# A decoder layer on one core: the attention loop's order, its division, its leads and an extra matmul

## The chip, the cores and the metric

The kernel runs on one core of a Trainium2 chip. The metric is the device time of one execution in microseconds; the time of a kernel is the median of several executions.

## The reference, cut to what matters

Input `x` and context are 8 batches of 256 tokens of 256 features (2048 tokens in all). Three sublayers follow each other, each with a layer norm ahead of it and a residual sum behind it.

```
x = x + mixer(layernorm(x))          # linear, depthwise conv, silu, decays by cumprod/cumsum, gates
q = layernorm(x) @ WQ + bQ; k = ctx @ WK + bK; v = ctx @ WV + bV      # 16 heads of 16
scores = where(causal, q k^T * 0.25, -inf); out = softmax(scores) @ v
x = x + out @ WO + bO
xn = layernorm(x); probs = softmax(xn @ router_w.T)        # 8 experts, top 2
rank = place of the pair within its expert; keep = rank < 641
h = silu(buf @ w1[e]); y = h @ w2[e]
x = x + (sum over k of k_prob * y[pair]) + xn
```

## The kernel before

The program has two parts with a barrier of all engines between them.

`mixer_and_projections` goes over four blocks (`NBLK`) of 512 tokens and makes the mixer's output, and the queries, keys and values of the attention. Large products are split: each fp32 operand is held as a high and a low part, and three products are summed (`split_product`, L101). Queries and keys are stored to HBM (`qd`, `kd`), values too (`vd`).

`attention_route_experts` has a loop over steps `t` (`for t in range(END)`), written out for each engine, and behind it the experts. The attention is cut into 16 groups `g` (`GR`: a batch and a half of its heads), each of three units: queries of the first 128 tokens with their keys (s = 0), and two units of later queries with all keys. There are 48 units (`NS`). Each unit is worked on twice:

- As a *lead*: `mask` (L243) and `scores` (L268) write scores of a unit `u` into `lead.sbank`, and VectorE's `maxima` (L282) reduces them to the negative row maxima's source. After the third unit of a group `turn_maxima` (L290 to L295) splits and transposes the maxima, SP stores them to HBM (`store_maxima`, L214) and loads them back as two more rows of the laid queries (`load_maxima`, L222).
- As a *turned* unit: `turned_mask` (L243) and `turned` (L1504) write the transposed scores less their maxima into `tbank`, ScalarE's `exps` (L1397) makes the exponentials, and `weigh` (L1522) multiplies with the values into `obank`.

The lead runs ahead of the turned unit by `LEAD` steps: in step `t` unit `u = t + LEAD` is masked and scored. The first `LEAD` units are done at the end of the mixer part, by `unit(u)` on TensorE and `maxima` on VectorE, placed by hand among the last block's products. `mask` waits for the maxima of the unit before it (`A["nm"]`), since there is one score buffer. The operands of a group are laid out in SBUF by four DMAs (`lay`, L207) into one of four places (`ITEMS`), when the last turned unit of the group four before has been read.

In the loop TensorE's order in a step is: turned mask of t, mask of u, turned scores of t, scores of u, then what is due (output projection `project` L1538 for a batch, the transposes `x3_turn` L1550, router `logits` L1560, `ranks` L1570), then `weigh(t - 1)`. What is due follows from constants: a batch's work at step `PROJECT + 6 b`, a block's at `constant + 12 i`.

VectorE's order is: maxima, turning of the maxima in each third step, `divide` of a group in each third step (transpose L1663, reciprocal L1665, multiplication L1667, transpose L1671), `x2` with the residual sum (L1678) and the statistics (L1681), `offset`, `choose` (best two of the router's logits, the gates), `place` (ranks to slots), and in each sixth step a piece of expert 0's second weights (`split_w2`, L1735, L1737). GpSimd adds the output bias at the start (L1317), takes inverse roots (`power`, L1321), adds the base (L1326), scatters the tokens to `disp` (L1335) and splits pieces of expert 0's first weights (L1342). ScalarE has the exponentials and, among them, normalised rows, copies and `high_w1`.

SP issues all other DMAs in one order: for each group from 2 on `lay(g + 2)`, `store_maxima(g)`, `load_maxima(g)`; behind group 3's the whole weights of expert 0 (two DMAs of 1 MB, L1264, L1267), behind group 6's those of expert 1; values (L233) and the stores of the base (L1278) at others.

Behind the loop the experts run one after the other, with TensorE's products L101 and L1613.

## Time and profile before

| what | value |
|---|---|
| median of 3 runs | 759.76 us (755.79 to 762.71) |
| profiled execution: its own time | 765.45 us |
| profiled execution: span | 763.7 us, 12738 instructions |
| mean granted TensorE clock | 0.866 |
| TensorE busy | 631.9 us, 83% |
| TensorE weight loads | 537.9 us, 70% |
| VectorE busy | 511.6 us, 67% |
| ScalarE busy | 340.3 us, 45% |
| GpSimd busy | 323.1 us, 42% |

The span is that of one profiled execution, from its first to its last instruction; its own time is a little longer. Busy shares are means over stages with different limits: the mixer to about 277 us, the attention loop to 440 us, the routing of the last block to about 475 us, the experts to the end. In the rows below a line begins with its start and its length in us; L and a number is the line of the kernel; in brackets stands how long the engine was idle before it and what ended that. PE is TensorE (PEld its weight loads), DVE VectorE, ACT ScalarE, POOL GpSimd, SPq the DMA issues of SP. The granted clock is a share of 2.4 GHz.

### The profile page before, as it was taken

What the parts mean: (1) busy time and instruction counts of PE and PEld (TensorE: products, weight loads), DVE (VectorE), ACT (ScalarE), POOL (GpSimd) and SP (SyncE); (2) the same over time, 40 slices, a digit from 0 to 9 for tenths busy, and PEclk for the clock granted to TensorE, in tenths of its full rate; (3) what the DMA queues carried; (4) which work ended last, traced back from release to release, by engine and by line L of the source; (5) the groups of instructions that cost most, each with busy time, mean ns of one, the idle gap of its engine ahead of it and who ended that gap; (6) DMA issues with size and microseconds to landing.
All of it is one profiled execution on the core that took longest, in us unless ns stands there. A gap on an engine that the chain in (4) does not pass through costs nothing.

```text
span 763.7 us, 12738 instructions
## 1 busy us (share of the span) xinstructions
PE 631.9 (83%) x4600; PEld 537.9 (70%) x4600; DVE 511.6 (67%) x1049; ACT 340.3 (45%) x658; POOL 323.1 (42%) x304
## 2 busy tenths in 40 slices
PE   3687989979976678679899751799999999999991
PEld 2465878867764645456566531699999999999991
DVE  5686787795785665775777741287777778777630
ACT  4565663742612123342342620356566555655540
POOL 1235433251430040020150637145867767677665
PEclk9798999999998665986676955699999999999996
DMA  9201305845229535775555201604253453521123
GB/s 285 80 26 43 99 28 158 258 117 151 70 54 269 120 86 102 221 206 119 120 130 136 83 11 42 214 1 148 29 164 57 132 148 46 162 27 19 19 30 41
DMA packets 60542, 81.16 MB, mean 106 GB/s; under 512 B 10188, under 2 KB 45015, under 8 KB 60481
## 3 DMA queue, kind: packets, MB, share of 16 engines
q1 hardware_dynamic: 51264, 72.55, 34.1%
q0 software_dynamic: 9216, 7.81, 7.2%
q8 instruction: 36, 0.59, 0.3%
q14 instruction: 26, 0.21, 0.1%
HBM read 48.01 MB, written 34.10 MB: 108 GB/s over the span
## 4 chain that ended last, share of the span: by engine, by line
PE 34%; issue 13%; POOL 6%; DMA 5%; SPq 2%; DVE 2%; ACT 1%; POOLq 0%; DVEq 0%
PE w_bank L1613 16%; PE w_bank L101 14%; POOL disp L1335 3%; DMA l_lo<-kd 3%; POOL out L1359 2%; PE l_scores L1582 1%; DMA md<-l_mt 1%; SPq L207 1%; PE a_shared L1538 1%; SPq L1259 1%; POOL l_lo L1348 1%; DMA w_rows<-disp 1%; DVE l_nm L282 1%; DMA out<-w_y,w_to 1%; POOL w_w1l L1342 0%
## 5 line engine op out<-in xcount | busy, mean ns | idle before, releaser
L1761 DVE SCALAR_TENSOR_TENSOR w_v<-w_th,w_bank 128x324 f32<-128x324 f32 x128 | 62.9, 491 | 71.1 <-ACT w_th L1430 69.8
L1613 PE MATMUL w_bank<-w_w2h,l_hi 128*108 128x256 f32 x384 | 108.6, 283 | 0.5 <-POOL l_lo L1348 0.5
L1613 PE MATMUL w_bank<-w_w2h,l_lo 128*108 128x256 f32 x384 | 107.7, 281 | 0.0
L1613 PE MATMUL w_bank<-w_w2l,l_hi 128*108 128x256 f32 x384 | 107.7, 280 | 0.0
L1430 ACT ACTIVATE w_th<-w_bank 128x324 f32<-128x324 f32 x128 | 56.5, 442 | 100.4 <-PE w_bank L101 100.3
L1348 POOL TENSOR_TENSOR l_lo<-w_v,l_hi 128x324 fp32r<-128x324 f32 x64 | 56.3, 880 | 91.8 <-ACT l_hi L1436 91.8
L1397 ACT ACTIVATE a_pr<-a_turned 128x1024 f32<-128x1024 f32 x48 | 49.1, 1023 | 96.8 <-PE a_turned L1504 96.8
L101 PE MATMUL w_bank<-l_hi,w_w1h 128*128 128x324 f32 x256 | 80.8, 316 | 1.1 <-ACT l_hi L1425 1.1
L101 PE MATMUL w_bank<-l_hi,w_w1l 128*128 128x324 f32 x256 | 80.9, 316 | 0.0
L1359 POOL DMA_INDIRECT out<-w_y,w_to x48 | 75.3, 1569 | 13.2 <-issue 9.9
L101 PE MATMUL w_bank<-l_lo,w_w1h 128*128 128x324 f32 x256 | 80.8, 316 | 0.0
L282 DVE TENSOR_REDUCE l_nm<-l_scores 128x4 f32<-128x1024 f32 (+1 forms) x48 | 58.1, 1211 | 33.1 <-PE l_scores L268 33.1
L1342 POOL TENSOR_TENSOR w_w1l<-w_s,w_w1h 128x256 fp32r<-128x256 f32 x64 | 57.0, 891 | 42.7 <-ACT w_w1h L1419 42.6
L1737 DVE TENSOR_TENSOR w_w2l<-w_s,w_w2h 128x256 fp32r<-128x256 f32 x64 | 65.5, 1024 | 2.2
L1613 PEld LDWEIGHTS w_bank<-w_w2h,l_hi 128*108 128x108 f32 x384 | 66.0, 172 | 0.9 <-issue 0.9
L1613 PEld LDWEIGHTS w_bank<-w_w2l,l_hi 128*108 128x108 f32 x384 | 65.9, 172 | 0.0
L1613 PEld LDWEIGHTS w_bank<-w_w2h,l_lo 128*108 128x108 f32 x384 | 65.9, 172 | 0.0
L1436 ACT ACTIVATE l_hi<-w_v 128x324 fp32r<-128x324 f32 x128 | 60.4, 472 | 12.0 <-DVE w_v L1761 11.1
L101 PEld LDWEIGHTS w_bank<-l_hi,w_w1h 128*128 128x128 f32 x256 | 49.1, 192 | 1.4 <-ACT l_hi L1425 1.4
L101 PEld LDWEIGHTS w_bank<-l_lo,w_w1h 128*128 128x128 f32 x256 | 49.2, 192 | 0.0
L101 PEld LDWEIGHTS w_bank<-l_hi,w_w1l 128*128 128x128 f32 x256 | 49.1, 192 | 0.0
L478 POOL TENSOR_TENSOR m_gl<-m_acc,m_gh 128x512 fp32r<-128x512 f32 x16 | 24.5, 1533 | 36.8 <-ACT m_gh L599 36.8
(229 smaller groups left out, 1541.6 us busy)
## 6 DMA issues: line engine op xcount, KB each, us to landing
w_s<-in_L_ffn_w SPq DMA_DIRECT2D x16, 1024.0 KB, 5.3
l_hi<-qd SPq DMA_DIRECT2D x32, 192.0 KB, 4.4
l_lo<-kd SPq DMA_DIRECT2D x32, 192.0 KB, 4.9
disp<-c_blank SPq DMA_DIRECT2D x8, 658.1 KB
w_rows<-disp SPq DMA_DIRECT2D x8, 658.1 KB
kd<-l_qkh SPq DMA_DIRECT2D x16, 256.0 KB, 4.7
vd<-m_vf SPq DMA_DIRECT2D x4, 1024.0 KB, 7.0
qd<-l_qkh SPq DMA_DIRECT2D x16, 256.0 KB, 5.0
```

Of the source, the lines that this page charges most:

```text
L101: mm = pe.matmul(out, a, b, start=first and n == 0, stop=last and n == 3 * len(parts) - 1)
L282: dve.tensor_reduce(dst, src, AX.X, ALU.max).then_inc(A["nm"], 1)
L478: pool.tensor_tensor(out[:, n, :], src, high[:, n, :].bitcast(F32), ALU.subtract).then_inc(S[name], 1)
L1342: pool.tensor_tensor(w1_piece(w1l, f), w1_piece(s1[e % 2], f), w1_piece(w1h, f).bitcast(F32), ALU.subtract)\
L1348: pool.tensor_tensor(hl[:, g % 3, half(1)], v[:, n % 4, :], hh[:, g % 3, half(1)].bitcast(F32), ALU.subtract)\
L1359: pool.indirect_dma_start(out=out, out_offset=bass.IndirectOffsetOnAxis(ap=to[:, e % 3, t:t + 1], axis=0), in_=y[e % 2][:, t, :], in_offse ...
L1397: act.activation(pr[n % 3][:, :], tbank[:, :], ACT.Exp, scale=SCALE).then_inc(A["exp"], 1)
L1430: act.activation(th[:, n % 2, :], hb[n % 3][:, 0:HALF], ACT.Tanh, scale=0.5).then_inc(F["th"], 1)
L1436: act.activation(hh[:, g % 3, half(u)], v[:, n % 4, :], ACT.Copy).then_inc(F["hh"], 1)
L1613: mm = pe.matmul(eb[t // 2][0:SP_, (t % 2) * D:(t % 2 + 1) * D], a[:, g % 3, s], w2_piece(b, f), start=f == 0 and t % 2 == 0 and n == 0, s ...
L1737: dve.tensor_tensor(w2_piece(w2l, f), w2_piece(s2[e % 2], f), w2_piece(w2h, f).bitcast(F32), ALU.subtract)\
L1761: dve.scalar_tensor_tensor(v[:, n % 4, :], th[:, n % 2, :], 1.0, hb[n % 3][:, 0:HALF], ALU.add, ALU.mult).then_inc(F["v"], 1)
```

## The change

- `LEAD` is 6 instead of 7. The six leading units get other places: unit 0 stood ahead of the last block's first products (`queries` of block 2, the projection `w2`), now it stands behind `w2`, and each of the others one place on; VectorE's maxima and their turning likewise. In SP's order laying group 1 moves behind the stores of block 2's queries. GpSimd takes the inverse root of block 2 ahead of four memsets instead of behind them.
- `divide` is cut: `invert` on VectorE (transpose, reciprocal), the multiplication on GpSimd (`divide`), and `turn_back` on VectorE one step later. One output bank instead of two; the x3 transposes get a bank of their own (`xbank`).
- The routing pieces get new steps, and the statistics and the gates are cut off from `x2` and `choose`.
- `keep_warm`: at the head of 36 of the 48 steps (all with t mod 12 not in 8, 9, 10) TensorE does one matmul of bf16 identity by 512 columns into `xbank`, whose result nothing reads.
- Expert 0's weights come in eight pairs of pieces of 128 KB (`first_weights`) in the groups with odd numbers, expert 1's behind group 14's maxima. The loads of the router's and the output projection's weights move behind group 2's maxima, and the last queries are stored in two halves with the maxima's load between them.

```diff
-LEAD = 7
+LEAD = 6
@@ mixer, sync
                     if i == NBLK - 1:
                         lay(sp, A, S, lead, qd, kd, 0)
-                        lay(sp, A, S, lead, qd, kd, 1)
+                lay(sp, A, S, lead, qd, kd, 1)
+                load_values(sp, A, S, lead, vd, 0)
                 lay(sp, A, S, lead, qd, kd, 2)
-                load_values(sp, A, S, lead, vd, 0)
                 lay(sp, A, S, lead, qd, kd, 3)
@@ mixer, tensor
-                    if i == NBLK:
-                        unit(0)
...
                     if last:
                         w2(i - 1)
                     if i == NBLK:
-                        unit(1)
+                        unit(0)
...
-                unit(6)
+                unit(5)
@@ mixer, vector
-                maxima(dve, A, lead, 6)
-
+                maxima(dve, A, lead, 5)
+                turn_maxima(dve, A, own, lead, 1)
@@ loop
-    PROJECT, BOTH, NORM, TURN, LOGITS, RANKS, SEND = 8, 14, 16, 18, 22, 24, 26
+    PROJECT, STATS = 8, 10
+    POWER, OFFSET, NORM, TURN, BASE, LOGITS = 17, 18, 19, 20, 21, 22
+    CHOOSE, RANKS, WEIGHTS, PLACE, SEND = 25, 26, 27, 31, 32
@@ sync
+                def first_weights(f):
+                    ge(sp, F["w1h"], f - 1)
+                    sp.dma_start(w1_piece(s1[0], f), w1[0:D, f * P:(f + 1) * P].rearrange("(k p) f -> p k f", p=P))                        .then_inc(F[f"p1_{f % 2}"], 16)
+                    ge(sp, F["w2l"], f - 1)
+                    sp.dma_start(w2_piece(s2[0], f), w2[f * P:(f + 1) * P, :]).then_inc(F[f"p2_{f % 2}"], 16)
...
-                    if g == 3:
-                        weights(0)
-                    if g == 6:
...
+                    if g % 2 == 1:
+                        first_weights(g // 2)
+                    if g == GR - 2:
                         weights(1)
@@ gpsimd
+                def divide(g):
+                    pool.wait_ge(A["po"], g + 1)
+                    pool.wait_ge(A["rc"], g + 1)
+                    ge(pool, A["o"], g)
+                    pool.tensor_tensor(on[:, :].rearrange("p (j h v) -> p h j v", h=2, v=HD), po[:, :, :, 0:HD],
+                                       rc[:, :, :].unsqueeze(3).to_broadcast([P, 2, 2 * 4, HD]), ALU.mult).then_inc(A["on"], 1)
@@ tensor
+                def keep_warm(t):
+
+                    if t % 12 in (8, 9, 10):
+                        return
+                    if t >= 23:
+                        pe.wait_ge(S["xt"], 2 * ((t - 23) // 12 + 1))
+                    pe.matmul(xbank[:, :], c["identb"][:, :], c["identb"][:, :].unsqueeze(1).to_broadcast([P, 4, P]),
+                              start=True, stop=True, skip_group_check=True)
...
                 for t in range(END):
                     u = t + LEAD
                     if t < NS:
+                        keep_warm(t)
                         turned_mask(t)
@@ vector
-                def divide(g):
+                def invert(g):
+                    dve.wait_ge(A["pv"], 3 * g + 3)
+                    ge(dve, A["on"], g)
+                    dve.transpose(po[:, :, :, :].rearrange("p h j r -> p (h j r)"), obank[:, :]).then_inc(A["po"], 1)
+                    dve.wait_ge(A["po"], g + 1)
+                    dve.reciprocal(rc[:, :, :], po[:, :, :, HD]).then_inc(A["rc"], 1)
+
+                def turn_back(g):
...
+                    dve.wait_ge(A["on"], g + 1)
                     ge(dve, S["y"], b - 1)
                     dve.transpose(ot[:, k, (b % 2) * L:(b % 2 + 1) * L], on[:, :]).then_inc(A["o"], 1)
...
                     if t % 3 == 0 and 1 <= t // 3 <= GR:
-                        divide(t // 3 - 1)
+                        invert(t // 3 - 1)
+                    if t % 3 == 1 and 1 <= t // 3 <= GR:
+                        turn_back(t // 3 - 1)
```

How the instructions now stand, at three places. TensorE, a step t with t mod 3 = 1 (step 4) of the loop: `a_turned` is the turned scores' bank, `l_scores` the leads', `a_out` the weighed values'. Before:

```order
970 L243 MATMUL a_turned<-c_identb,c_laterT 128x2x64 [waits a_exp]
971 L243 MATMUL a_turned<-c_identb,c_laterT 128x2x64 x3
972 L243 MATMUL l_scores<-c_identb,c_later 128x2x64 [waits a_nm]
973 L243 MATMUL l_scores<-c_identb,c_later 128x2x64 x3
974 L1504 MATMUL a_turned<-l_hi,l_lo 128x256 x4
975 L268 MATMUL l_scores<-l_lo,l_hi 128x256 x4
976 L1522 MATMUL a_out<-a_pr,l_hi 32x256 [waits a_v_in0,a_exp]
```

and of the change:

```order
971 L1516 MATMUL a_turned_x<-c_identb 128x512
972 L243 MATMUL a_turned<-c_identb,c_laterT 128x2x64 [waits a_exp]
973 L243 MATMUL a_turned<-c_identb,c_laterT 128x2x64 x3
974 L243 MATMUL l_scores<-c_identb,c_later 128x2x64 [waits a_nm]
975 L243 MATMUL l_scores<-c_identb,c_later 128x2x64 x3
976 L1534 MATMUL a_turned<-l_hi,l_lo 128x256 x4
977 L268 MATMUL l_scores<-l_lo,l_hi 128x256 x4
978 L1552 MATMUL a_out<-a_pr,l_hi 32x256 [waits a_v_in0,a_po,a_exp]
```

The extra matmul stands between the last weighing and the turned mask that waits for the exponential, and the weighing that begins a group now waits for `a_po`, the first transpose of the group before it.

VectorE, steps 6 to 8 of the loop. Before, with the whole division behind the maxima of step 6:

```order
306 L282 TENSOR_REDUCE l_nm<-l_scores 128x2x2 [waits a_s]
307 L1663 STREAM_TRANSPOSE a_po<-a_out 128x512 [waits a_pv]
308 L1665 RECIPROCAL a_rc<-a_po 128x16 [waits r_step]
309 L1667 TENSOR_TENSOR a_on<-a_po,a_rc 128x2x8x16 [waits r_step]
310 L1671 STREAM_TRANSPOSE a_ot<-a_on 128x256 [waits r_step]
311 L282 TENSOR_REDUCE l_nm<-l_scores 128x2x2 [waits a_s]
312 L290 CAST l_mx<-l_nm 128x16 [waits a_mx,a_nm]
313 L292 TENSOR_TENSOR l_mx<-l_nm,l_mx 128x16 [waits r_step]
314 L295 STREAM_TRANSPOSE l_mt<-l_mx 128x32 [waits a_md,r_step]
315 L282 TENSOR_REDUCE l_nm<-l_scores 128x8 [waits a_s]
316 L1678 TENSOR_TENSOR g_x<-a_shared,g_x 128x512 [waits w_y,w_xb]
```

and of the change:

```order
306 L282 TENSOR_REDUCE l_nm<-l_scores 128x8 [waits a_s]
307 L1688 STREAM_TRANSPOSE a_po<-a_out 128x512 [waits a_on,a_pv]
308 L1690 RECIPROCAL a_rc<-a_po 128x16 [waits a_po]
309 L282 TENSOR_REDUCE l_nm<-l_scores 128x2x2 [waits a_s]
310 L1696 STREAM_TRANSPOSE a_ot<-a_on 128x256 [waits a_on]
311 L282 TENSOR_REDUCE l_nm<-l_scores 128x2x2 [waits a_s]
312 L290 CAST l_mx<-l_nm 128x16 [waits a_mx,a_nm]
313 L292 TENSOR_TENSOR l_mx<-l_nm,l_mx 128x16 [waits r_step]
314 L295 STREAM_TRANSPOSE l_mt<-l_mx 128x32 [waits a_md,r_step]
315 L1702 TENSOR_TENSOR g_x<-a_projected,g_x 128x512 [waits w_y,w_xb]
```

The multiplication has left VectorE, the second transpose stands a step later, and the turning of the maxima moved from the second to the third step of a group.

SP, behind group 2's maxima. Before, where `w_s` is the experts' weights and 1 MB each:

```order
108 L214 DMA md<-l_mt 4x32x32 [waits a_mx]
109 L222 DMA l_hi<-md 2x1024 [waits a_md]
110 L222 DMA l_hi<-md 2x1024
111 L1264 DMA w_s_0<-in_L_ffn_w 128x2x1024
112 L1267 DMA w_s_0<-in_L_ffn_w 128x8x256
113 L207 DMA l_hi<-qd 48x4x256 [waits a_st]
```

and of the change:

```order
111 L214 DMA md<-l_mt 4x32x32 [waits a_mx]
112 L222 DMA l_hi<-md 2x1024 [waits a_md]
113 L222 DMA l_hi<-md 2x1024
114 L1267 DMA w_s_0<-in_L_ffn_w 128x2x128
115 L1269 DMA w_s_0<-in_L_ffn_w 128x256
116 L207 DMA l_hi<-qd 48x4x256 [waits a_st]
```

The two large loads have become two small ones at the same place.

## Rows read from the trace of the kernel before

**Rows 1.** Stretches: us, us, busy PE, PEld, DVE, ACT, POOL; clock, DMA share, GB/s.
```profile
277.00:440.00 163.00, 137.11 (x1458) 90.20 (x1456) 112.50 (x267) 59.70 (x76) 40.58 (x33) 0.74 0.56 141
...
486.00:745.00 259.00, 258.53 (x1986) 257.93 (x1985) 184.94 (x367) 146.44 (x368) 169.76 (x161) 0.99 0.34 79
```

**Rows 2.** The exponentials: duration ns min/median/max, first and last start us.
```profile
L1397 ACT ACTIVATE a_pr<-a_turned x48: 1003/1023/1026, 277.5 to 439.9; 128x1024 f32<-128x1024 f32 x48
```

**Rows 3.** Waits in 277 to 440: us in total, times, longest.
```profile
PE l_scores L243 <- DVE l_nm L282: 9.3, 16, 1.1
...
PE l_scores L268 <- DMA l_lo<-kd: 5.6, 3, 2.8
...
PE a_out L1522 <- DMA l_lo<-vd: 2.0, 1, 2.0
```

**Rows 4.** Timeline of TensorE, steps at the low and at the high clock.
```profile
297.92 0.40 PE L243 MATMUL a_turned<-c_identb,c_laterT 64*128 64x128 bf16 x4
...
300.59 0.40 PE L243 MATMUL a_turned<-c_identb,c_laterT 64*128 64x128 bf16 x4
...
376.11 0.29 PE L243 MATMUL a_turned<-c_identb,c_laterT 64*128 64x128 bf16 x4
...
377.92 0.29 PE L243 MATMUL a_turned<-c_identb,c_laterT 64*128 64x128 bf16 x4 [0.31 <-ACT a_pr L1397]
379.27 0.29 PE L243 MATMUL l_scores<-c_identb,c_later 64*128 64x128 bf16 x4 [1.07 <-DVE l_nm L282]
...
379.69 0.40 PE L268 MATMUL l_scores<-l_lo,l_hi 48*128 48x256 f32 x4
...
380.97 0.39 PE L243 MATMUL a_turned<-c_identb,c_laterT 64*128 64x256 bf16 x4 [0.31 <-ACT a_pr L1397]
382.41 0.61 PE L243 MATMUL l_scores<-c_identb,c_later 64*128 64x256 bf16 x4 [1.04 <-DVE l_nm L282]
...
394.45 1.99 PE L1538 MATMUL a_shared<-w_wo,a_ot 128*128 128x256 f32 x8
...
402.53 0.61 PE L243 MATMUL a_turned<-c_identb,c_laterT 64*128 64x256 bf16 x4
...
406.10 0.40 PE L243 MATMUL a_turned<-c_identb,c_laterT 64*128 64x128 bf16 x4
```

**Rows 5.** Timeline of VectorE, the division's ends and the maxima behind it.
```profile
379.13 0.71 DVE L1663 STREAM_TRANSPOSE a_po<-a_out 128x512 f32<-128x512 f32 x1
...
380.80 0.45 DVE L1671 STREAM_TRANSPOSE a_ot<-a_on 128x256 f32<-128x256 f32 x1
381.16 1.19 DVE L282 TENSOR_REDUCE l_nm<-l_scores 128x4 f32<-128x1024 f32 x1
```

**Rows 6.** Timelines of VectorE and TensorE, the mixer's end, ahead of w2.
```profile
237.51 1.28 DVE L954 TENSOR_TENSOR m_xal<-m_ssm,m_xah 128x512 fp32r<-128x512 f32 x2
...
240.03 1.12 PE L268 MATMUL l_scores<-l_lo,l_hi 48*128 48x128 f32 x8 [3.62 <-DMA l_lo<-kd]
```

**Rows 7.** SP's issues around group 4's maxima, and its waits for all groups.
```profile
305.22 1.36 SPq L207 DMA_DIRECT2D l_hi<-qd  x2
...
307.95 0.55 SPq L214 DMA_DIRECT2D md<-l_mt  x1
316.58 0.57 SPq L222 DMA_DIRECT2D l_hi<-md  x2
...
SPq L222 <- DMA md<-l_mt: 58.0, 15, 8.4
```

**Rows 8.** Two operations by line: duration ns min/median/max, first and last start.
```profile
L1667 DVE TENSOR_TENSOR a_on<-a_po,a_rc x16: 424/425/2236, 290.0 to 443.5; 128x256 f32<-128x256 f32 x16
...
L1342 POOL TENSOR_TENSOR w_w1l<-w_s,w_w1h x8: 720/734/877, 310.0 to 453.2; 128x256 fp32r<-128x256 f32 x8
```

**Rows 9.** Timeline of VectorE, the gates of the last block.
```profile
462.25 0.18 DVE L1710 TENSOR_SCALAR w_one<-w_ex 128x4 f32<-128x4 f32 x1
...
462.95 0.17 DVE L1716 TENSOR_TENSOR w_x<-w_wr,w_x 128x4 f32<-128x4 f32 x1
```

149 lines of the change are left out of this document (74 added, 75 removed).

## The prediction

> **What bounds the kernel now.** I read the table of stretches first, then the waits and the timelines of the attention loop. The loop runs from 277 to 440 us, and in it TensorE is busy 137 of 163 us at a mean granted clock of 0.74 [rows 1]. The clock has two levels, 1.2 and 2.4 GHz, so 0.74 is (1 - 0.74) / 0.5 = 52% of the time at the lower one: 85 us. The experts behind it (486 to 745 us) run at 0.99 with TensorE busy throughout; the change leaves them alone. So the time has to come from the loop, from the mixer's end ahead of it, or from the routing tail behind it.
>
> The 48 exponentials start between 277.5 and 439.9 us [rows 2], 162.4 / 47 = 3.46 us a step, and last 1.02 us each: ScalarE is not the bound. One step is a ring of four engines. TensorE masks and makes scores, VectorE takes their maxima, TensorE may only then mask the next scores; and since its queue is in order, the turned scores of the next step, and so the next exponential, stand behind that mask. TensorE's own waits are 9.3 us for VectorE, 5.6 us for keys and 2.0 us for values [rows 3].
>
> At the high clock a narrow step is short: mask at 376.11, next mask at 377.92, 1.81 us, of which the last 0.31 us is the wait for the exponential [rows 4]. At the low clock the same step goes from 297.92 to 300.59, 2.67 us, without any wait. In the step after 377.92 the mask waits 1.07 us, because the division (from 379.13) and the maxima stand one behind the other on VectorE: the division's four operations fill 379.13 to 381.25 [rows 5]. After two steps with waits of 0.31, 1.07 and 1.04 us the matmuls at 382.41 are at the lower clock [rows 4]. The waits thus cost twice: as waits, and as a slow array for the steps behind them.
>
> **The mixer's end.** Unit 0 stood ahead of the projection w2 in TensorE's queue and held it 3.62 us for its keys, until 240.03; it ended at 241.15. The inputs of w2 are ready when VectorE's two subtractions from 237.51 end, 1.28 us later, at 238.79 [rows 6]. Unit 0 now stands behind w2, so w2 starts 241.15 - 238.79 = 2.4 us earlier, and the chain to the barrier with it. Given back: the six leading units end with both VectorE's maxima and their turning (three small operations like those of [rows 9], taken at 0.6 us), and a turning also stands ahead of the normalisation (0.6 us). Net -1.0 us, bounds -3 and +1. One unit fewer ahead of the loop costs nothing in it by itself: its last steps had no scores to make, now the last six rather than seven.
>
> **Waits for transfers.** 5.6 + 2.0 = 7.6 us [rows 3]. The laying of an item waits for the turned scores of the item four before it, as before, and its scores now come one step later (six leading units), one more step of 2 to 3 us for the transfer. The two loads of 2 MB each for experts 0 and 1 stood in the queue ahead of it: with one ahead, the small store of maxima issued at 307.95 let its load go only at 316.58, 8.6 us, where SP's fifteen waits of this kind are 3.9 us in the mean [rows 7]. Expert 0's weights now come in eight pairs of pieces, and expert 1's at the last items but two. I take -6 us. New costs: fourteen more issues on SP, and the last maxima store behind expert 1's 2 MB, +1 us. Together -5.0 us, bounds -8 and +3.
>
> **VectorE's pieces.** The division's multiplication goes to GpSimd, its second transpose one step on; statistics, choice, gates and placing get steps of their own; and with six leading units the turning of the maxima falls in a step without division. A step's surplus beside the maxima falls from 2.1 us [rows 5] to about 0.4 to 1.0 us, which fits beside TensorE's mask, turned scores and scores. Not in all steps: choice, the split of w2 and the placing still overrun. Of 9.3 us of waits I take half, -4.5 us, bounds -9 and 0. On GpSimd a subtraction of the same 128x256 takes 0.73 us against 0.42 us on VectorE [rows 8]; it has a whole step there and hides. A single output bank replaces two: the next item's first weighing waits for the first transpose, which is a step earlier.
>
> Here a rule of the Trainium skill speaks against the change: SBUF — State Buffer, section "SBUF: two separate sides", says that VectorE and GpSimd share one port pair, which an instruction holds alone, so that a GpSimd operation blocks VectorE's operations with two SBUF inputs. The trace agrees that such a thing occurs: this division's multiplication takes 0.425 us in the median and 2.236 us at most [rows 8]. By the rule sixteen divisions of 0.73 us on GpSimd could return up to 12 us; but what stands behind the reciprocal on VectorE is the maxima, which read PSUM.
>
> **The filler.** 48 steps less 12 skipped (three in each twelve) are 36 matmuls of 512 columns. None like it is in the trace. The nearest are the masks, in bf16 too: four of 256 columns, two and two side by side, stream 512 columns in 0.61 us at the low clock (402.53) and in 0.39 us at the high one (380.97) [rows 4], the end of the last one included. Half the clock costs 0.22 us more, so the columns themselves are 0.22 us at the high and about 0.43 us at the low clock, which I take; bounds 0.2 and 0.6. In the 0.31 us wait of a fast narrow step it costs nothing. In steps where TensorE is the bound, as when the output projection runs (1.99 us at the high clock [rows 4]), it is added: 8 fast steps, +2 us. In slow steps, which have no wait, it is added whole.
>
> What it buys is the clock. A slow narrow step is 2.67 us, a slow wide one, each third, 406.10 - 402.53 = 3.57 us [rows 4]; the mean is 2.97, and 85 us at the low level are 29 slow steps. I take that 10 stay slow: those at the loop's start, and those behind the logits. Then 19 steps change level. Each gains 2.67 - 1.81 = 0.86 us at most, but at the high clock the ring of the maxima (1.19 us [rows 5]) plus mask, turned scores and scores (379.27 to 380.09 [rows 4], 0.8 us) and its hops binds at about 2.1 us, so 0.5 us each: -9.5 us. The ten slow ones pay 10 x 0.43 = +4.3 us. Bounds for the clock part with the filler: -16 us (no slow step left, 29 x 0.55) and +12.5 us (29 stay, 29 x 0.43).
>
> **The tail.** The division through GpSimd adds 0.3 us and a hop, +0.5 us; the gates of block 2, four small operations of 0.9 us (462.25 to 463.12 [rows 9]), now stand between the last sum and its statistics, +0.9 us. The 16 scatters on GpSimd were already end to end, and the first waits a little longer for the placing that moved to this place. I take +1.5 us, bounds 0 and +4.
>
> **Sum.** -1.0 - 5.0 - 4.5 + 2.0 - 9.5 + 4.3 + 1.5 = -12.2 us. On the profiled execution, 765.45 us (span 763.7), this is 753.2. The median of the runs shown is 759.76, 5.7 us below the profiled one, with 755.79 to 762.71 among three. Part of that 5.7 us may be stalls and clock that I count as gain. Against the median the sum gives 747.6; I forecast 747. What a measurement of this kernel can tell from no change is about 1%, 7.6 us; the forecast is past it by 5 us.
>
> **Rivals.** First, the array stays fast through the whole loop and VectorE's load is even: clock part -16 instead of -9.5 + 4.3, waits -7, giving -1 - 5 - 7 + 2 - 16 + 1.5 = -25.5: 734. For it: after full projections and transposes the clock rose each time. Against: the step at 297.92 had no wait and was slow all the same. Chance 0.22.
>
> Second, the other sign: the filler does not lift the clock. It stands in 29 slow steps at 0.43 us, +12.5, and in slow steps VectorE's waits are covered anyway, so their 4.5 us are not gained: -1 - 5 + 12.5 + 1.5 = +8: 768. It decides from about 21 slow steps of the 29: without VectorE's gain the sum is -1 - 5 + 1.5 - 0.5 x (29 - N) + 0.43 x N, which is zero at N = 20.4. For it: the step at 297.92 ran without any wait and stayed slow. Against: the falls come behind waits that the change shortens. Chance 0.13.
>
> Third, SP's queue becomes the bound: laying 2.7 (305.22 to 307.95), store 0.55, wait 3.9 less the issue's 0.5, load 0.57 [rows 7] and the added pieces 0.6 us on the mean make about 7.8 us for three steps, against some 8.5 us wanted. If the store's landing rises to 6 us, three steps take 10 us, 14 items 140 us, and the loop ends near 434: -6 + 1.5: 755. For it: the queue waits 8.6 us where much is under way [rows 7]. Against: the big loads are cut up. Chance 0.2. By the port rule above, a fourth: VectorE's two-input pieces in steps with a division (gates, placing) each lose up to 0.73 us, 12 us at the very most and 1 to 2 us likely: 749, chance 0.05, inside the forecast's own range.
>
> **Numbers.** Forecast 0.4 (own range 741 to 753), fast rival 0.22, slow 0.13, queue 0.2, port 0.05. The 8 in 10 range reaches from 729 to 767. Faster by over 1% (below 752.2): the fast rival, most of the forecast and the port case, a little of the queue, 0.63; within 1%: 0.23; slower by over 1%: 0.14.
>
> **What would show it.** The exponentials should span about 150 us instead of 162.5, and TensorE's mean clock in the loop be 0.85 to 0.92. The waits for keys should be gone except near the last items, those of the mask for VectorE be near 0.4 us each, w2 start near 239, and the tail be longer by 1 to 2 us. If the clock stays at 0.75 the filler step is wrong; if the clock rises and the loop still takes 160 us, a new wait, most likely for the maxima's load, has come in; if the experts' stretch changes, nothing here accounts for it.

## The result and the profile after

The changed kernel runs at a median of 754.4 us (750.89 to 759.39, 20 runs) beside 762.22 us for the kernel before (755.79 to 769.95, 20 runs): a recorded ratio of 0.9914, 95% interval [0.9894, 0.9934] (the quotient of the two medians is 0.9897). Timed once more, beside some of its variants, it took 752.21 us (749.63 to 754.36, 6 runs), where the kernel before took 761.61 in the same job: 0.9868 [0.9833, 0.9904]. By the medians it is faster by 8 to 9 us. The forecast was 747, with 729 to 767 as its range: the direction was right, the time lies 5 to 7 us above the forecast, and the gain is 8 to 9 us where I had forecast 12.8.

The profiled execution took 752.78 us, with a span of 751.1. The first view is that of the stretches, with the columns of [rows 1], cut at the first and last exponential, at one common point of the experts' start, and at the end. First the kernel before, once as recorded ahead of the prediction and once from a second profiled execution of the same kernel:

```profile
277.50:439.90 162.40, 136.51 (x1448) 89.64 (x1448) 112.43 (x266) 59.57 (x75) 40.08 (x33) 0.74 0.56 142
439.90:489.70 49.80, 19.31 (x111) 15.04 (x112) 13.41 (x66) 7.43 (x17) 19.86 (x19) 0.50 0.29 93
489.70:763.70 274.00, 257.17 (x1991) 256.38 (x1989) 185.33 (x368) 147.29 (x371) 180.72 (x168) 0.97 0.33 73
```

```profile
276.90:436.00 159.10, 137.66 (x1448) 90.33 (x1448) 112.46 (x266) 59.50 (x76) 40.15 (x33) 0.72 0.58 145
436.00:486.10 50.10, 19.23 (x111) 14.96 (x108) 13.38 (x65) 7.34 (x17) 19.88 (x19) 0.50 0.30 93
```

Then the changed kernel, its first profile and its second:

```profile
275.20:422.90 147.70, 130.70 (x1495) 83.34 (x1497) 102.15 (x241) 59.70 (x74) 41.02 (x41) 0.84 0.59 146
422.90:477.10 54.20, 19.21 (x112) 15.14 (x112) 13.99 (x76) 7.53 (x16) 28.09 (x28) 0.53 0.35 113
477.10:751.10 274.00, 256.58 (x1991) 255.79 (x1990) 185.49 (x368) 147.46 (x371) 181.50 (x168) 0.98 0.33 73
```

```profile
277.10:425.60 148.50, 135.17 (x1495) 86.20 (x1497) 102.15 (x242) 59.58 (x74) 41.24 (x41) 0.80 0.57 145
425.60:478.10 52.50, 19.18 (x111) 15.13 (x112) 13.69 (x75) 7.55 (x16) 27.81 (x28) 0.53 0.36 115
```

The experts take 274.0 us in both kernels, so the whole difference lies ahead of them. In the mean of two profiles the first exponential comes 1.0 us sooner (277.5 and 276.9 before, 275.2 and 277.1 now), the loop is 12.7 us shorter (160.75 to 148.1) and the tail 3.4 us longer (49.95 to 53.35). Of the first profile's tail, 2.8 us are a pause of VectorE that the second does not have, ahead of the placing of the last block and released by nothing in the program:

```profile
450.48 0.23 DVE L1752 TENSOR_TENSOR w_tmp<-a_routing,w_hot 128x64 f32<-128x64 f32 x1 [2.78 <-remote]
```

So I take the second profile for the tail: 2.5 us longer than in the kernel before. GpSimd is busy for 28 us of it, where it was busy for 20.

TensorE's waits between the first and the last exponential, in place of [rows 3] (engine, line, what it waited for: us in total, times, longest):

```profile
PE l_scores L243 <- DVE l_nm L282: 6.8, 14, 1.4
PE a_out L1552 <- DMA l_lo<-vd: 4.6, 3, 3.3
PE a_turned L1534 <- DMA l_hi<-md: 4.3, 1, 4.3
```

The wait for keys is gone, as forecast. The wait for VectorE fell from 9.3 to 6.8 us (in the second profiles of the two kernels from 9.4 to 5.4), and 4.3 us for the maxima and 4.6 us for values (4.2 and 1.9 in the second profile) stand where 2.0 us for values stood. Both new waits come from SP's queue. Its timeline (`md` are the maxima in HBM, `vd` the values, `w_s` the experts' weights):

```profile
299.16 0.56 SPq L214 DMA_DIRECT2D md<-l_mt  x1
303.44 0.55 SPq L222 DMA_DIRECT2D l_hi<-md  x2
...
306.24 1.25 SPq L207 DMA_DIRECT2D l_lo<-kd  x2
307.53 0.55 SPq L214 DMA_DIRECT2D md<-l_mt  x1
312.00 0.56 SPq L222 DMA_DIRECT2D l_hi<-md  x2
...
400.60 0.47 SPq L1276 DMA_DIRECT2D w_s<-in_L_ffn_w  x1
401.11 1.40 SPq L233 DMA_DIRECT2D l_lo<-vd  x1
```

The store at 307.53 lets its load go 4.47 us later; in [rows 7] the same pair took 8.6 us, and with the weights whole again, in a run below, it takes 8.47. That is the cut-up weights at work. But the queue now has less time to spare: it waited 0.4 us in all for TensorE to free an item's place (5.0 us in the second profile), where it waited 18.7 us in the kernel before (17.1 in its second profile). And the last values are issued right behind the 2 MB of expert 1. TensorE shows where both waits end:

```profile
305.27 0.80 PE L1534 MATMUL a_turned<-l_hi,l_lo 50*128 50x256 f32 x4 [4.35 <-DMA l_hi<-md]
...
410.25 1.08 PE L1552 MATMUL a_out<-a_pr,l_lo 128*32 128x256 f32 x8 [3.29 <-DMA l_lo<-vd]
...
412.56 3.50 PE L1565 MATMUL a_projected<-w_wo,a_ot 128*128 128x256 f32 x8
```

Behind either wait the array is at the low clock. The three steps behind the first run at 0.50, and behind the second the eight matmuls of the projection take 3.50 us, where the same took 1.99 us in [rows 4].

### The profile page after: what moved, and what is told of

Same layout as the page of the kernel before. It is cut to its first block and busy times, and to the rows that moved or that the text cites. A ratio compares the mean times of both kernels' runs of the same rounds, so it can differ in the third digit from the quotient of the medians.

```text
span 751.1 us, 12854 instructions
## 1 busy us (share of the span) xinstructions
PE 624.7 (83%) x4636; PEld 530.7 (71%) x4636; DVE 501.0 (67%) x1033; ACT 340.8 (45%) x658; POOL 333.7 (44%) x320
## 5 line engine op out<-in xcount | busy, mean ns | idle before, releaser
L1457 ACT ACTIVATE l_hi<-w_v 128x324 fp32r<-128x324 f32 x128 | 60.5, 473 | 11.9 <-DVE w_v L1791 11.1
L1344 POOL TENSOR_TENSOR a_on<-a_po,a_rc 128x256 f32<-128x256 f32 x16 | 10.0, 622 | 93.3 <-DVE a_rc L1690 57.0
```

Source lines behind the costliest of these rows:

```text
L1344: pool.tensor_tensor(on[:, :].rearrange("p (j h v) -> p h j v", h=2, v=HD), po[:, :, :, 0:HD], rc[:, :, :].unsqueeze(3).to_broadcast([P, 2 ...
L1457: act.activation(hh[:, g % 3, half(u)], v[:, n % 4, :], ACT.Copy).then_inc(F["hh"], 1)
```

## The experiments

Eighteen runs were made, four of them repeats of a kernel. "Loop" is from the first to the last of the 48 exponentials in the one profiled execution of a run, with its granted clock; "low" is (1 - clock) / 0.5 of it, the time at the lower level. Two profiles of one kernel differ by up to 4 us in the loop. The medians are of 6 to 12 runs, apart from the last row, and twice the standard error of the difference between two of them is 2 to 3.5 us: differences under 3 us are told apart barely or not at all.

| kernel | median us | ratio to before, 95% | loop us, clock | low us | tail us |
|---|---|---|---|---|---|
| changed, second time | 752.21 | 0.9868 [0.9833, 0.9904] | 148.5, 0.80 | 59 | 52.5 |
| no matmul | 756.77 | 0.9925 [0.9891, 0.9960] | 153.7, 0.69 | 95 | 53.6 |
| no matmul, second time | 756.36 | 0.9937 [0.9911, 0.9964] | 149.9, 0.72 | 84 | 53.0 |
| matmul twice | 749.51 | 0.9807 [0.9764, 0.9851] | 147.1, 0.87 | 38 | 52.5 |
| matmul three times | 747.03 | 0.9811 [0.9771, 0.9851] | 143.6, 0.94 | 17 | 52.0 |
| weights whole | 761.84 | 1.0001 [0.9973, 1.0029] | 156.3, 0.81 | 59 | 53.1 |
| store ahead of laying | 746.43 | 0.9778 [0.9742, 0.9814] | 144.2, 0.82 | 52 | 52.6 |
| values early | 748.78 | 0.9828 [0.9785, 0.9870] | 143.5, 0.86 | 40 | 51.0 |
| WO's loads ahead | 751.21 | 0.9844 [0.9808, 0.9880] | 150.9, 0.81 | 57 | 52.7 |
| division whole | 753.32 | 0.9865 [0.9824, 0.9906] | 154.3, 0.80 | 62 | 51.3 |
| division whole, second time | 753.04 | 0.9892 [0.9854, 0.9931] | 154.3, 0.79 | 65 | 51.3 |
| routing early, last two blocks | 753.28 | 0.9876 [0.9838, 0.9914] | 150.1, 0.81 | 57 | 53.2 |
| routing early, all | 749.25 | 0.9826 [0.9792, 0.9860] | 147.5, 0.86 | 41 | 50.7 |
| that, and nothing spread | 751.82 | 0.9849 [0.9814, 0.9884] | 154.3, 0.81 | 59 | 50.1 |
| three parts | 738.63 | 0.9690 [0.9655, 0.9725] | 131.5, 0.97 | 8 | 52.2 |
| six parts | 733.84 | 0.9622 [0.9596, 0.9649] | 133.8, 0.96 | 11 | 49.6 |
| before, store ahead of laying | 761.01 | 0.9977 [0.9947, 1.0008] | 158.5, 0.76 | 76 | 49.8 |
| before, one run | 761.80 | | 159.1, 0.72 | 89 | 50.1 |

All but the last two are the changed kernel or edits of it. The base for differences is its second time, 752.2. I expected 754 to 756 for it, and the rival, 751 to 753, held; most expectations below were written against the first, 754.4. Against that one each gain is 2.2 us larger and each loss 2.2 us smaller.

**Was my base a slow one?**

> The kernel before, unchanged, for a second profiled execution. Theory (my sum was made on an execution that was slow for its kernel): the span of this one lies nearer to the kernel's usual 760 to 762 us than the 763.7 of the first profile, its mean granted clock is above 0.866, and the stretch from the first to the last of the 48 exponentials is under 162.5 us by the same 2 to 4 us. Rival (the first profile was typical, and the sum itself is off): the stretch is again 162 to 163 us, and nothing of my error lies in the base.

The loop took 159.1 us: 3.3 less than in the profile I had read, as the theory said, but the clock was 0.865, not above 0.866, so half of that expectation failed. What differs is a wait: TensorE waited 2.9 us for keys, where it was 5.6 in the first profile. The kernel before spreads that much between executions. In the run by run record of the changed kernel, time and clock go together (0.901 at 750.89 us, 0.885 at 759.39 us), with a correlation of -0.72 over 20 runs; the clock thus goes with about half of the variance in time.

**The matmul: none, one, two, three.**

```
-                        keep_warm(t)
```

> The changed kernel without the 512-column matmul. Theory (the sum of the prediction): the matmul gives back some 9.5 us of clock and costs 6.3, so without it the kernel is slower by about 3 us: near 757.5, the 48 exponentials span 150 to 152 us instead of 147.7, and the granted clock of the stretch is 0.72 to 0.78 instead of 0.83. Rival 1 (the matmul is worth more, since it is nearly free in the wait for the exponential): slower by 8 us or more, clock under 0.75. Rival 2 (the clock comes from the waits that went, the matmul only costs): 2 to 6 us faster, clock still above 0.80.

> The changed kernel without the 512-column matmul, again. The prediction's term: 3 us slower than the changed kernel in this same job. Rival (one matmul costs at the low clock, 3.00 to 3.27 us or more a step, about what it gives back in steps at the high clock; only the second pays): within 1.5 us of it.

> The changed kernel with two of the 512-column matmuls in each of the 37 steps that have one. The first costs 0.32 to 0.34 us from its start to the next instruction in a step at the high clock. Theory (TensorE's queue is the bound of a step at the high clock, so every column in it is paid): the second costs 25 steps x 0.33 = 8 us and 12 slow steps x 0.54 = 6 us less what the clock returns on them (at most 12 x 0.6 = 7): near 761, slower by 5 to 10 us. Rival (the wait for the exponential has room for two): within 2 us of the changed kernel.

> The changed kernel with three of the 512-column matmuls in each of the 37 steps. With one and with two a step at the high clock takes 2.30 us alike; at the low clock it took 3.00 us with none, 3.27 to 3.58 with one and 3.69 to 4.00 with two. Theory (at the high clock the exponential's cycle is the bound, and of the 1.28 us between two exponentials some 0.3 us is left after two matmuls; at the low clock each is paid in full): 2.30 to 2.45 us a step at the high clock, 4.2 to 4.5 at the low one, the kernel within 3 us of the 749.5 of two. Rival (the queue fills at three): 2.6 us or more a step at the high clock and 755 or more in all.

Without it the kernel is 4.2 us slower in one job (756.36 against 752.21), near the 3.2 forecast. Against the first measurement of the changed kernel the same variant was only 0.1% away in the ratio, which is why both were run again side by side. Over all runs, 19 without and 26 with it, the means differ by 2.5 us, give or take 1.4. The low time tells more: without the matmul it is 95 and 84 us, as in the kernel before (84 and 89), and 47 and 59 us with it; over whole executions the clock is 0.861 to 0.873 in the 19 runs without it and 0.884 to 0.903 in the 26 with it. So the shorter waits alone did not lift the clock; the matmul did. It stands in 36 steps, not the 37 that my expectations name. My expectation for two was wrong: not 761 but 749.5. The exponentials show why. First the second to the fourth exponential without the matmul, then the same with one, then the second and third with two, all at the granted clock of 0.50, and last the second to the fourth with three, at 1.00:

```profile
278.29 1.02 ACT L1418 ACTIVATE a_pr<-a_turned 128x1024 f32<-128x1024 f32 x1 [1.63 <-PE a_turned L1534]
281.33 1.02 ACT L1418 ACTIVATE a_pr<-a_turned 128x1024 f32<-128x1024 f32 x1 [2.02 <-PE a_turned L1534]
284.23 1.02 ACT L1418 ACTIVATE a_pr<-a_turned 128x1024 f32<-128x1024 f32 x1 [1.87 <-PE a_turned L1534]
```
```profile
277.87 1.02 ACT L1418 ACTIVATE a_pr<-a_turned 128x1024 f32<-128x1024 f32 x1 [1.62 <-PE a_turned L1534]
281.46 1.02 ACT L1418 ACTIVATE a_pr<-a_turned 128x1024 f32<-128x1024 f32 x1 [2.56 <-PE a_turned L1534]
284.72 1.02 ACT L1418 ACTIVATE a_pr<-a_turned 128x1024 f32<-128x1024 f32 x1 [2.24 <-PE a_turned L1534]
```
```profile
278.01 1.02 ACT L1418 ACTIVATE a_pr<-a_turned 128x1024 f32<-128x1024 f32 x1 [1.62 <-PE a_turned L1534]
282.02 1.02 ACT L1418 ACTIVATE a_pr<-a_turned 128x1024 f32<-128x1024 f32 x1 [2.99 <-PE a_turned L1534]
```
```profile
277.51 1.02 ACT L1418 ACTIVATE a_pr<-a_turned 128x1024 f32<-128x1024 f32 x1 [1.27 <-PE a_turned L1534]
279.95 1.02 ACT L1418 ACTIVATE a_pr<-a_turned 128x1024 f32<-128x1024 f32 x1 [1.42 <-PE a_turned L1534]
282.24 1.02 ACT L1418 ACTIVATE a_pr<-a_turned 128x1024 f32<-128x1024 f32 x1 [1.26 <-PE a_turned L1534]
```

At the low clock the step is 3.04, 3.59 and 4.01 us: each matmul is paid, some 0.4 to 0.55 us. At the high clock a step with nothing else due is 2.30 us with none, one or two, and 2.30 to 2.45 with three. So in such a step the matmul costs nothing at the high clock, and a step that changes level saves 0.7 us of the 3.00 it takes without the matmul, or 1.1 of the 3.4 with it.

What sets the 2.30 is not the exponential's cycle, as several of my expectations say. In the last six steps no scores are left to make, and those of them with nothing else due take 1.70 us. It is the ring of the maxima, which VectorE's rows show (with the matmul twice):

```profile
325.94 1.23 DVE L282 TENSOR_REDUCE l_nm<-l_scores 128x8 f32<-128x1024 f32 x1 [1.43 <-PE l_scores L268]
327.08 0.71 DVE L1689 STREAM_TRANSPOSE a_po<-a_out 128x512 f32<-128x512 f32 x1
327.82 0.26 DVE L1691 RECIPROCAL a_rc<-a_po 128x16 f32<-128x16 f32 x1
328.09 1.23 DVE L282 TENSOR_REDUCE l_nm<-l_scores 128x4 f32<-128x1024 f32 x1
```

TensorE's next mask follows at 329.37, 0.05 us behind the second reduction's end, and its scores end at 330.39: 1.23 + 0.05 + 1.02 = 2.30. Without the matmul the step is as long, and the mask then stands idle for 0.21 to 0.32 us before the maxima are done.

**The expert weights in pieces.**

```
-                    if g % 2 == 1:
-                        first_weights(g // 2)
-                    if g == GR - 2:
+                    if g == 3:
+                        weights(0)
+                    if g == 6:
                         weights(1)
```

Besides these lines the first pair of pieces, ahead of the loop, goes, and the splits of the second weights come six steps later.

> The changed kernel with the first expert's weights loaded whole behind item 3 and the second's behind item 6, as in the kernel before, and the splits of w2 a step pair later. Theory (the 2 MB transfers hold up the 256 KB layings of the items behind them; in the kernel before TensorE waited 5.6 us for kd): waits for kd or md come back behind steps 6 to 20, 4 to 7 us in all, and the kernel is near 759. Rival (with TensorE's faster steps the transfers are no later than before and only the wait for vd at the end goes): 751 to 755.

9.6 us slower than the changed kernel (7.4 by its first time), and level with the kernel before. This is the largest part of the change. TensorE's waits:

```profile
PE a_turned L1530 <- DMA l_hi<-md: 7.7, 2, 4.1
PE l_scores L243 <- DVE l_nm L282: 6.6, 13, 1.4
PE a_out L1548 <- DMA l_lo<-vd: 6.1, 1, 6.1
```

It is the maxima and the values that come late behind 2 MB, 13.8 us, no longer the keys. In the changed kernel's second profile the same two waits are 6.1 us, and the 7.7 between them are the loop's (156.3 against 148.5), at the same 59 us of low time. The run undoes two things at once, and the steps tell them apart. Behind expert 0's weights the twelfth step takes 6.88 us where it took 3.27. Behind expert 1's, which stand at item 6 instead of 14, values come 6.1 us late and the twentieth and twenty-first take 9.00 and 5.84 us where they took 2.30 and 3.89; the forty-fourth and forty-fifth give 2.5 us back. So in this profile moving expert 1's loads to the end was worth more (6.2 us) than cutting expert 0's (3.6).

**The order in SP's queue.**

```
-                    if g + 2 < GR:
-                        lay(sp, A, M, lead, qd, kd, g + 2)
                     store_maxima(sp, A, lead, md, g)
+                    if g + 2 < GR:
+                        lay(sp, A, M, lead, qd, kd, g + 2)
                     load_maxima(sp, A, lead, md, g)
```

> The changed kernel with the store of item g's maxima issued ahead of the laying of item g + 2, in place of behind it. Theory (SP's queue, which in the changed kernel never waits for a place to come free, is late for the steps that wait for md at the ninth step, 4.3 us, and sets the rate of others): the wait for md goes, the ninth step falls from 8.45 us to about 4.5, and the kernel is 3 to 6 us faster, near 750. Rival 1 (the loop is bound by the cycle exponential - corners - turned scores - exponential, 2.30 us at the high clock, and SP only follows): within 1.5 us of 754.4, the ninth step stays above 7 us. Rival 2 (SP's queue is the bound of the whole loop, as the third case of the prediction had it): 10 us or more faster.

> The kernel before with the store of item g's maxima issued ahead of the laying of item g + 2. Theory (in the kernel before SP waited 18.7 us for TensorE to free places, so its queue was not short of time, and the edit only pays in the changed kernel): within 2 us of 762. Rival (the store behind the laying was a cost of the kernel before too): 4 us or more faster. Second rival (the laying comes later and the wait for kd grows): slower.

> The changed kernel with the loads of the router's weights and of WO again ahead of the loop (behind the second item's maxima), as in the kernel before. Theory (these nine loads stand in SP's queue between item 2's and item 3's maxima and are why the ninth step takes 8.45 us with a 4.3 us wait for md): the ninth step takes 4 to 5.5 us and the kernel is 3 to 5 us faster than 754.4, near 750. Rival (the nine loads delay the layings and maxima wherever they stand; SP's order is the cause): the wait for md appears at another step before the tenth and the time is within 1.5 us.

> The changed kernel with each batch's values loaded one item earlier (behind the maxima of item 2b - 1), so that the last ones no longer stand behind the 2 MB of the second expert's weights. Theory (the 3.3 us wait for vd at 410.25 is on the path and drops the clock for the two steps behind it, 5.65 and 4.95 us): the wait goes, the two steps take about 4 and 4 us, the kernel is 3 to 4 us faster, near 751. Rival (the loads land late anyway because the queue's bandwidth is shared, or the wait moves to the second expert's weights or to the maxima): within 1 us.

The store ahead of the laying gives 5.8 us, at the upper end of the first theory (8.0 against the 754.4 that it was written for, past that end). The ninth step falls from 8.45 to 4.14 us, since the laying now fills the store's landing:

```profile
294.58 0.57 SPq L214 DMA_DIRECT2D md<-l_mt  x1
295.26 1.55 SPq L207 DMA_DIRECT2D l_hi<-qd  x2
296.85 1.25 SPq L207 DMA_DIRECT2D l_lo<-kd  x2
298.15 0.75 SPq L222 DMA_DIRECT2D l_hi<-md  x2
```

In the kernel before, the same edit gives 0.8 us with an interval that holds no change: there SP waited 17 to 19 us for TensorE and had time to spare. So SP's order is a cost that the change uncovers. Moving back the nine loads of the router's weights and WO moved the wait and did not remove it: a step of 8.51 us appears three steps sooner, with a wait of 5.7 us for md, and the time is 1.0 us off. In the steps the rival held; against the 754.4 of the expectation the time is 3.2 us off, which is the theory's, so the time decides nothing. The values one item earlier give 3.4 us, as expected (5.6 against 754.4, more than expected); the forty-fourth and forty-fifth steps, 5.65 and 4.95 us in the changed kernel's first profile and 3.60 and 4.71 in its second, take 2.22 and 3.63.

**VectorE's pieces.** In the first (run twice) the division's product goes back to VectorE and all of it into one step; in the second the statistics go back too, and the routing stands early as in "routing early, all" below. One line of the second:

```
-PROJECT, STATS = 8, 10
+PROJECT, STATS = 8, 8
```

> The changed kernel with the division whole on VectorE again, in one step, as in the kernel before (transpose, reciprocal, product, transpose back). Theory (the split takes 0.7 us a division off VectorE in a step whose mask waits for VectorE's maxima): 14 steps get back a wait of 0.5 to 0.9 us, the loop is 4 to 8 us longer and the kernel near 760; the waits of the masks for l_nm grow from 7 to 12 us or more. Rival (the exponential's cycle of 2.30 us hides it; the split only lengthens the tail by GpSimd's queue): within 1.5 us of 754.4, the tail a microsecond shorter.

> The changed kernel with the division whole on VectorE, again. The prediction's term: 3 to 4.5 us slower than the changed kernel in this same job. Rival: within 1.5 us of it, since what the loop loses (3.12 us in place of 2.30 in seven steps) the tail gives back (51.3 us in place of 54.2).

> The same kernel as the one with the routing steps of all blocks early, with the statistics again in the step of the sum (8 in place of 10) and the division whole on VectorE: nothing of VectorE's work is spread any more. Theory of the prediction (the waits for VectorE that go are worth 4.5 us): 4 to 6 us slower than the kernel with the early steps alone. Rival (at the high clock a step is bound by the exponential's cycle and most of these waits lie in steps that the transfers or the projection stretch anyway; the division alone was worth nothing): within 1.5 us of it.

The division whole costs 0.8 us by the medians (753.04 against 752.21); over all 13 runs with it and 26 without it the means differ by -0.2 us, give or take 1.9. The steps that hold it do take 3.12 us at the high clock in place of 2.30, and the masks wait 10.0 and 8.9 us for VectorE in place of 6.8 and 5.4; in the profiles the loop is 6 us longer and the tail 1 to 3 shorter, but these two profiled executions took 4 to 5 us more than the median of their kernel, and in the medians most of it does not show. With nothing spread it is 2.6 us slower than with early routing alone, give or take 3.5. And that kernel, in which none of VectorE's work is spread any more, takes 751.82 us, no more than the changed one: what it loses in the loop its tail, 2.4 us shorter, gives back. The term of 4.5 us was too large.

**The tail.**

```
+            early = {CHOOSE: 22, RANKS: 24, WEIGHTS: 24, PLACE: 25}
```

The scatters (`SEND`) go from 32 to 26.

> The changed kernel with the routing steps of the last two blocks (choice, ranks, gates, places, scatters) at the offsets of the kernel before: 22, 24, 24, 25, 26 in place of 25, 26, 27, 31, 32. Theory (the tail is 4.5 us longer because block 2's places and scatters start only behind the last exponential and run into block 3's): from the last exponential to the first copy for the experts 42.5 to 44 us instead of 46.8, the whole 2.5 to 4 us faster, near 751. Rival (the tail's extra comes from the work of VectorE and GpSimd that the loop leaves, however the constants stand): the tail stays above 46 and the time within 1 us of 754.4. Second rival: the tail shortens, but the loop's last steps pay it back in waits for VectorE (the 48 exponentials span 149 us or more).

> The changed kernel with the routing steps of all four blocks at the offsets of the kernel before (22, 24, 24, 25, 26); in the run that did this for the last two blocks alone, GpSimd's scatters of the second block stood in the tail, ahead of the reciprocal root that the last block waits for, and the tail stayed 3.4 us above the kernel before. Theory (GpSimd's queue behind the last exponential is what lengthens the tail by 4.4 us): with the second block's scatters back in the loop the tail is within 1 us of the kernel before's 49.8 us, and the kernel is 3 to 4 us faster than the changed one if the loop pays nothing. Rival (the choice and places in VectorE's loop cost as much as the tail gains): tail near 50, the 48 exponentials 2 to 4 us longer, the whole within 1.5 us of 754.4. Second rival: the tail stays above 52.5.

With the last two blocks alone the tail stayed at 53.2 us and the time within 1.1 us of either base, so the theory failed: ten scatters, a division and two subtractions of GpSimd now stood between the last exponential and the last block's root, which started at 442.26 although its input was ready at 439.59. With all four blocks early the tail is 50.7 us and the kernel 3.0 us faster; the loop, at 147.5 us, pays nothing, so that no gain in the loop shows from the later steps of the choice, gates and places. The changed kernel's GpSimd in the tail, second profile, from the first scatter of block 2 to its last and the first of block 3:

```profile
440.81 1.04 POOL L1354 DMA_INDIRECT disp<-w_x,w_si  x1 [1.90 <-issue]
441.88 2.36 POOL L1338 TENSOR_TENSOR g_x<-g_x,w_x 128x1024 f32<-128x1024 f32 x1
...
452.11 0.98 POOL L1354 DMA_INDIRECT disp<-w_x,w_si  x1 [0.30 <-issue]
453.39 0.97 POOL L1354 DMA_INDIRECT disp<-w_x,w_si  x1 [0.30 <-issue]
```

Block 3's places are ready at 451.02, but block 2's scatters hold the queue until 453.09: its first scatter is 2.4 us late. In the kernel before that was 1.3 us (ready at 463.98, first scatter at 465.26).

**Together.** Store ahead of laying, values early, and the matmul twice; then, besides, two matmuls behind each block's logits, all routing early, and the bases' stores two items later.

> The changed kernel with three of the edits together: the store of the maxima ahead of the laying, the values one item earlier, and two of the 512-column matmuls a step. Alone they gave 8.0, 5.6 and 4.9 us against the changed kernel's 754.4. If they are independent: 736. Theory (they share the slow steps behind the ninth and the forty-fourth step, so that part of the clock is gained once): 738 to 743, no wait of TensorE for md or vd above 1 us, granted clock of the loop 0.92 or more, loop near 135 us. Rival (each only moves the same stretch of low clock elsewhere): 745 to 747, no better than the best alone.

> The three edits and three more: two 512-column matmuls behind each block's logits, the routing steps early for all blocks, and the stores of the first two blocks' bases at items 10 and 14 in place of 8 and 12. Theory: the step of the logits (5.05 us at a clock of 0.73) and the two or three slow ones behind it give back some 3 us for the blocks, the tail 3 us: 732 to 737. Rival (the logits' step drops the clock whatever follows it, and the choice back in the loop costs what the tail gains): within 1.5 us of the kernel with the three edits.

Both times fell into the ranges of their theories. With three, 42 of 47 steps are at the high clock, and one wait for md of 1.5 us is left, where I had expected none above 1. The edits' single gains of 5.8, 3.4 and 2.7 us (11.9) came to 13.6; against the first base they are 18.5 and came to 15.8. So the runs do not show whether the edits share slow steps, as the theory had it, or add up. The six show a shorter tail (49.6 against 52.2) and no shorter loop, so what the matmuls behind the logits give is not shown. With six the kernel runs at 733.84 us, 3.8% faster than the kernel before. The stretches of loop and tail, for three and for six:

```profile
275.50:407.00 131.50, 122.94 (x1532) 74.68 (x1532) 102.94 (x242) 59.60 (x75) 41.62 (x41) 0.97 0.67 164
407.00:459.20 52.20, 19.18 (x111) 15.12 (x112) 13.26 (x75) 7.55 (x17) 27.36 (x28) 0.53 0.36 118
```
```profile
278.90:412.70 133.80, 125.17 (x1534) 74.61 (x1536) 104.30 (x259) 59.52 (x74) 48.49 (x48) 0.96 0.70 170
412.70:462.30 49.60, 19.30 (x113) 14.75 (x114) 11.36 (x57) 7.45 (x17) 20.42 (x20) 0.53 0.32 102
```

## Why the prediction was right in direction and too large

The step that failed is the term for VectorE's pieces, "of 9.3 us of waits I take half, -4.5 us". The waits did fall, by 2.5 and 4.0 us in the two pairs of profiles, but the time did not follow: undone, the pieces cost 0.8 us (the division) and 2.6 us (all), and a kernel with none of them spread is, with its shorter tail, as fast as the changed one. Clear of noise is only that the division alone is worth less than 4.5 us; what takes the waits' place is not shown. Besides, the base was 2.5 us too low, and SP's new costs, at +1, were priced far too low; the gain from the transfers, priced too low as well, made up for that.

**The base (2.5 us).** The sum was worked out on an execution of 765.45 us and subtracted from a median of three, 759.76. Twenty runs put the kernel before at 762.22. The text said that part of the 5.7 us between the two might be stalls and clock counted as gain; the forecast then took off all of it. From 762.22 the same sum gives 750.0. The kernel took 2.2 to 4.4 us more than that, which is what the terms are off by: about 1 in the tail, the rest in the loop, if the -1.0 ahead of it is taken as it was forecast.

**The mixer's end, -1.0: the start of w2 held, the size is not resolved.** w2's matmuls start at 239.59, right behind VectorE's subtractions that end at 239.49. I had written "near 239". The first exponential comes 1.0 us sooner in the mean of two profiles, but single profiles have it anywhere from 274.7 to 278.9, so that the agreement may be luck.

**The loop, five terms with the sum -12.7.** The two pairs of profiles give -12.7 as well, but with a spread of some 3 us, and that agreement is luck; by the medians, with 1.0 ahead and 2.5 in the tail set off, it is -9.3 to -10.9. The parts were off by more than the sum.
- Transfers, -5.0: too small. The cut of expert 0's weights and the move of expert 1's are worth 7.4 to 9.6 us. I had counted the waits of the kernel before, 7.6 us, and not that in a faster loop the small loads of maxima and the values would be later behind 2 MB: 13.8 us.
- New costs of SP, +1: too small, and the second thing to name. The last values and the ninth step's maxima wait 3.3 and 4.3 us; the two edits that take these away give 3.4 and 5.8 us.
- VectorE's pieces, -4.5: too large, and the term that failed, as said above. That half of the waits would go was a guess that no row carried; as a count of waits it was near, as time it was not. The mask still waits 1.4 us where a surplus meets the maxima.
- The matmul where TensorE is the bound, +2.0, and where it is slow, +4.3 at 0.43 us each. The 0.43 was right (0.43 in the mean of the second to the fourth step). The 2.0 was too large. I counted eight steps with a projection, but in four of them (t mod 12 is 8) the matmul is left out: the twenty-first step, one of them, takes 3.89 us at the high clock with none, one, two or three matmuls. In the twenty-seventh it costs 0.32 us (3.87 against 3.55), and there are three such steps in the loop: about 1 us.
- The clock, 19 steps at 0.5 us, -9.5. The time at the low level fell from 84 and 89 us to 47 and 59, some 14 to 17 steps of 3.4 us, where I had left ten of 29 slow; without the matmul it did not fall at all. Each gains more than I took: 3.00 to 2.30 is 0.7, since I had the ring of the maxima at 2.1 and the slow step at 2.67 to 2.97. Fewer steps than the 19, each worth more: with the costs above, 2.0 to 4.2 us net by the two bases, 3.2 in the forecast. This mechanism held, though the loop's clock, 0.84 and 0.80, stayed below the 0.85 to 0.92 that I had written.

**The tail, +1.5: the mechanism I priced held, a second was missed.** From the last exponential to the last block's offset it is 13.3 us in the second profile, where it was 11.9: the 1.4 us that division and gates were priced at. I also wrote that GpSimd's scatters were already end to end and that the first waits a little longer. It does, and with the base's addition the eight of block 2 keep block 3's back 1.1 us more than before. Together +2.5, inside the bounds; the run that moves the routing back gives 3.0 us.

**The rivals.** The fast one (734) did not happen with this change. Kernels with a loop's clock of 0.96 and 0.97 take 734 and 739 us, but they have lost waits for transfers besides, so they do not test its price. The second fell: the matmul lifts the clock, and without it the kernel is slower. The third named the right queue and, at 755, nearly the measured time; it was wrong about the extent. SP's queue does not set all steps (most take the ring's 2.30 us) but holds up a few, and behind these the clock is low: the tenth to the twelfth step run at 0.50, and at 1.00 with the store ahead of the laying. It deserved more than 0.2, and as a cost inside the forecast rather than a case beside it.

The fourth, the port rule, shows at the gates of block 2, VectorE's rows first and GpSimd's under them:

```profile
400.46 0.51 DVE L1744 TENSOR_TENSOR w_x<-w_ex,w_wr 128x4 f32<-128x4 f32 x1
401.00 0.65 DVE L1746 TENSOR_TENSOR w_x<-w_wr,w_x 128x4 f32<-128x4 f32 x1
```
```profile
400.33 0.62 POOL L1344 TENSOR_TENSOR a_on<-a_po,a_rc 128x256 f32<-128x256 f32 x1 [5.43 <-DVE a_po L1688]
400.91 0.72 POOL L1361 TENSOR_TENSOR w_w1l<-w_s,w_w1h 128x256 fp32r<-128x256 f32 x1
```

Operations that take 0.17 us in the gates of the last block of the same profile take 0.51 and 0.65 here, each ending within 0.02 us of the GpSimd operation beside it; the mask behind them waited 1.42 us. The trace agrees with the Trainium skill, SBUF — State Buffer, section "SBUF: two separate sides", by which such operations of the two engines exclude each other. It cost VectorE 0.8 us in this step, at the lower end of the 1 to 2 us that I had weighed for the loop; what it cost in others was not added up.

**What stays open.** The parts undone one at a time (9.6 for the weights, 4.2 for the matmul, 2.6 for the spread, less 3.0 for the late routing) make 13.4 us, more than the 8 to 9 of the whole. Each is uncertain by 2 to 3.5 us, and they may share slow stretches, so they need not add up; but six leading units, the single output bank and the unit behind w2 were not undone alone, and may cost a few us.

## What to carry to other kernels

Where an in-order array runs at two clock levels, first find the ring that sets a step at the high level; work put into its slack is free there, and what it is worth is read from the number of steps that change level. When transfers wait one behind the other in a queue that has no time to spare, put the small store that something waits for ahead of the big laying, and cut large transfers or move them to where nothing stands behind them, before balancing engines by tenths of a microsecond. An operation moved later in an order must be followed to the last round, where nothing hides it; and a sum made on one execution is to be set against the kernel's usual time, not against a luckier one.

## What was not expected of the hardware

- With three matmuls a step the loop starts at a granted clock of 1.00: TensorE's first step takes 2.30 us, where with one or two the first steps run at 0.50 to 0.66 and take 2.65 to 4.01 us. It waited 3.09 us just ahead of the loop in that run all the same. What makes the difference is not shown here.
- The clock falls behind a wait and not only in it: after the 3.29 us for values, two steps run at 0.66 and 0.70 and take 5.65 and 4.95 us, against 2.22 and 3.63 without that wait. The wait of 3.3 us thus cost 4.7 us of time in that execution.
- GpSimd does the division's product of 128x256 in 0.611 to 0.657 us in the first profile of the changed kernel, below the 0.72 of the nearest row I had.
